# A graph attention and the routing behind it in one stage, with masks made on VectorE and each routed row written with both gates

## The reference

```python
x = x + _L2_gnn_ref(_layernorm(x), adj, W, a)      # graph attention
    h = x @ W;  e = s_src[:, :, None] + s_dst[:, None, :]   # h @ a[:d], h @ a[d:]
    e = where(e >= 0, e, 0.2 * e);  e = where(A <= 0, -inf, e)
    y = softmax(e) @ h
x = x + _L2_ffn_ref(_layernorm(x), ...)            # 8 experts, top 2
    probs = softmax(xt @ Wr + br);  top_p, top_idx = top_k(probs, 2)
    weights = top_p / top_p.sum(-1)
    xn = layernorm(xt)                             # a second norm
    out = sum of weights * (gelu(xn * g + b @ W1 + b1) @ W2 + b2) of the two experts
x = x + _L3_gnn_ref(_layernorm(x), adj, W, a)      # graph attention again
x = x + _L3_ffn_ref(...)                           # heads over 192 tokens, then 8 gated experts, top 2
```

## Time and profile before

| | us |
|---|---|
| median of 3 runs | 5281.62 |
| lowest, highest | 5274.88, 5283.15 |
| profiled execution | 5278.31 |
| its span | 5276.6 |

### The profile page before, as it was taken

The page is one execution under the profiler, slowest core; times in us unless marked ns, Lnnn a source line. Parts: engine busy times, 40 slices in busy tenths (PEclk is TensorE's granted clock), DMA queues, the critical chain, the costliest instruction groups (busy, mean ns, idle before and its releaser), DMA issues. The chain is left out here.

```text
span 5276.6 us, 85946 instructions
## 1 busy us (share of the span) xinstructions
PE 3931.5 (75%) x25676; PEld 2536.8 (48%) x25676; DVE 2964.8 (56%) x10714; ACT 2064.0 (39%) x5230; POOL 1883.7 (36%) x1833
## 2 busy tenths in 40 slices
PE   3999978888888539999886776279565677751995
PEld 1333337777777313333364565157454344431563
DVE  5666644444444766666487887412388555552344
ACT  1666643333333006566532265234255344431331
POOL 3445410000000024554362174745575311236344
PEclk9999975555555659999998888589888899965997
DMA  4333348000000023333100021144431000001445
GB/s 130 107 103 115 97 170 374 0 0 0 0 0 0 0 76 100 112 107 101 32 0 1 5 100 33 47 123 148 144 103 33 1 0 0 0 21 49 130 128 160
DMA packets 237303, 376.21 MB, mean 71 GB/s; under 512 B 24832, under 2 KB 157056, under 8 KB 228672
## 3 DMA queue, kind: packets, MB, share of 16 engines
q1 hardware_dynamic: 218688, 336.03, 20.3%
q0 software_dynamic: 18432, 38.05, 2.1%
HBM read 210.37 MB, written 163.61 MB: 71 GB/s over the span
## 5 line engine op out<-in xcount | busy, mean ns | idle before, releaser
L1343 DVE CUSTOM_DVE_ANT_0 mha_seen<-mha_score,mha_mask 128x512 f32<-128x512 f32 x1024 | 686.4, 688 | 456.5 <-PE mha_score L1114 453.4
L1246 ACT ACTIVATE mha_prob<-mha_turned 128x512 f32<-128x512 f32 x1024 | 608.8, 601 | 489.5 <-PE mha_turned L1125 459.1
L1114 PE MATMUL mha_score<-mha_k_rows,mha_q_rows 96*128 96x512 bf16 x1024 | 397.0, 390 | 58.3 <-DMA mha_k_rows<-split_rows 29.8
L3025 POOL DMA_INDIRECT expert_rows<-expert_y,expert_target x320 | 306.3, 957 | 368.4 <-DVE expert_y L3160 150.6
L1124 PE MATMUL mha_turned<-mha_maskT,core_ident_bf 128*128 128x512 bf16 x1024 | 392.4, 383 | 4.0 <-ACT mha_prob L1246 3.5
L1125 PE MATMUL mha_turned<-mha_q_rows,mha_k_rows 99*128 99x512 bf16 x1024 | 390.3, 381 | 0.0
L1498 PE MATMUL lstm_gates<-lstm_h_part,lstm_w_part 128*128 128x16 f16 x4608 | 271.4, 179 | 123.6 <-DVE lstm_h_part L1660 123.5
L1448 POOL TENSOR_TENSOR core_mid<-lstm_hist,lstm_per_unit 128x256 f32 x32 | 23.5, 733 | 942.8 <-DVE lstm_hist L1661 942.8
L1498 PEld LDWEIGHTS lstm_gates<-lstm_h_part,lstm_w_part 128*128 128x128 f16 x4608 | 231.2, 109 | 211.4 <-DVE lstm_h_part L1660 164.2
L1491 PE MATMUL lstm_gates<-lstm_xg,core_ident 128*128 128x48 f32 x1024 | 327.9, 420 | 0.7 <-ACT lstm_xg L1566 0.7
L2698 POOL DMA_INDIRECT routed_rows<-route_rows,core_slot x256 | 254.1, 993 | 149.8 <-issue 82.6
(11 more groups left out here) (477 smaller groups left out, 9282.3 us busy)
## 6 DMA issues: line engine op xcount, KB each, us to landing
routed_rows<-lstm_blank SPq DMA_DIRECT2D x66, 1040.0 KB, 25.0
core_params<-adj SPq DMA_DIRECT2D x32, 1024.0 KB, 5.9
gat_adj_raw<-adj SPq DMA_DIRECT2D x32, 1024.0 KB, 5.4
mha_q_rows<-split_rows SPq DMA_DIRECT2D x64, 384.0 KB, 4.5
mha_k_rows<-split_rows SPq DMA_DIRECT2D x64, 384.0 KB, 5.5
expert_x<-routed_rows SPq DMA_DIRECT2D x80, 260.0 KB
expert_w<-weights SPq DMA_DIRECT2D x80, 256.0 KB
combine_pair<-expert_rows SPq DMA_DIRECT2D x32, 512.0 KB, 4.9
```

The source lines that it names most:

```text
L1114: pe.matmul(score[n % 2][:, :], rows[0][s][0:ROWS, h, t * P:(t + 1) * P], rows[1][s][0:ROWS, h, :], start=True, stop=True).then_inc(S["sco ...
L1246: act.activation(prob[:, n % RING, :], turned[n % 2][:, :], ACT.Exp, scale=-1.0).then_inc(S["prob_ready"], 1)
L1343: dve.tensor_tensor_reduce(seen[n % 2][:, :], score[n % 2][:, :], mask[1 - s][:, t, :], 1.0, 3e38, ALU.add, ALU.min, low[g][:, t, j:j + 1] ...
L3025: pool.indirect_dma_start(out=core.y_rows[NUMBER][:, :], out_offset=bass.IndirectOffsetOnAxis(ap=target[q][:, t:t + 1], axis=0), in_=y_buf ...
```

## The change

- The first routing becomes part of the first graph attention: `gat_stage(core, 5, 2, route=6)`, with a class Router that holds the routing's steps. The loop over graphs runs 22 iterations instead of 16. In iteration b (where the index exists) POOL normalises graph b + 2, makes the scales of graph b - 1 (11 operations of 128x4, two of them powers, in place of DVE's bit trick over all graphs), and from iteration 6 on writes half a group, 8 DMAs, of group b // 2 - 3. PE turns and rates graph b - 2 between its attention matmuls; ACT scales the rows of graph b - 1 straight into the rows to be written. DVE makes the mask of b + 2, then the mark step of a group in odd iterations from 5, the pick step in even ones from 4, takes the logits of b - 2, then does out(b).
- Masks are made on DVE in both graph attentions, ahead by two graphs (L2671 of the changed kernel).
- zlow has one PSUM bank instead of two, in both graph attentions: ACT's lower of tile t waits for DVE's leak of tile t - 1. The other bank holds the counts.
- Each token has one row in SBUF, and both writes take it. ROW is 132: 128 features, the mark, the second slot's line, the lower gate, and the difference of the gates. The expert stages find out by comparing the line with their own index which of the two gates is meant (four more operations of 128x4 a tile on DVE, one iota and one addition at the start).
- The second routing loses copy_rows on ACT and the copy L2841 on DVE; ACT normalises into a ring of three groups.
- SP waits for four semaphores of written rows instead of two. The blanked buffer is larger by 132/130.

(In the diff: first the sizes and two of the Router's methods, then the buffers, the programs of POOL, PE, ACT and DVE in gat_stage in that order, then POOL in route_stage, DVE in expert_stage and the program.)

```diff
-ROW = D + 2
+ROW = D + 4
...
+    def scales(self, pool, b):
+        chain.step(pool.tensor_scalar(arg, var, LN_EPS, None, ALU.add))
+        chain.step(pool.tensor_scalar(shift, mean, -1.0, None, ALU.mult))
+        chain.settle()
+        chain.step(pool.tensor_tensor(scale, arg, half, ALU.pow))
+        chain.settle()
...
+    def normal(self, act, b):
+        act.wait_ge(S["r_scaled"], b + 1)
+        if g >= self.RING:
+            act.wait_ge(self.sent[s], 16 * 2 * self.R * (g // self.RING))
+        for t in range(T):
+            ins = act.activation(self.rows[s][:, i * T + t, 0:D], self.core.x_res[:, b, t, :], ACT.Identity, ...)
...
-        zlow = [m.ps(f"zlow{n}") for n in range(2)]
+        zlow, count_ps = m.ps("zlow"), m.ps("count_ps")
+        rate_ps = [s_ps[:, (2 + n) * T * E_:(3 + n) * T * E_] for n in range(2)]
+        router = Router(m, core, route, S) if route else None
+        LAST = B + 5 if route else B - 1
...
             need(pool, "stat_done", STATS[False])
             normalise(0)
-            forbid(0)
             normalise(1)
-            for b in range(B):
-                if b + 1 < B:
-                    forbid(b + 1)
+            if route:
+                router.constants(pool)
+            for b in range(LAST + 1):
                 if b + 2 < B:
                     normalise(b + 2)
+                if route and 0 <= b - 1 < B:
+                    need(pool, "stat_out", b)
+                    router.scales(pool, b - 1)
+                if route and b >= 6:
+                    half = b % 2 * T
+                    router.scatter(pool, b // 2 - 3, range(half, half + T))
...
+            for b in range(LAST + 1):
+                if route and 5 <= b < B + 5 and b % 2:
+                    router.count_picked(pe, (b - 5) // 2, count_ps)
+                if b < B:
+                    back(b, 0)
+                    back(b, 1)
+                    values(b, 0)
+                if routed:
+                    route_turn(b - 2)
+                if b < B:
+                    back(b, 2)
+                    values(b, 1)
+                if routed:
+                    route_rate(b - 2)
...
-                need(act, "leaky", T * b + t - 1)
+                need(act, "leaky", T * b + t)
...
+                if route and 0 <= b - 2 < B:
+                    router.take_turned(act, b - 2, row_ps)
...
+                if route and 0 <= b - 1 < B:
+                    router.normal(act, b - 1)
...
+            forbid(0)
+            forbid(1)
             masked(0)
...
                         leak(b + 1, t)
-                out(b)
+                if b + 2 < B:
+                    forbid(b + 2)
+                if route and 5 <= b < B + 5 and b % 2:
+                    router.mark_rows(dve, (b - 5) // 2, count_ps)
+                if route and 4 <= b < B + 4 and b % 2 == 0:
+                    router.pick(dve, b // 2 - 2)
+                if route and 0 <= b - 2 < B:
+                    router.take(dve, b - 2, rate_ps[b % 2])
+                    if b % 2:
+                        router.lower_logits(dve, (b - 3) // 2)
+                if b < B:
+                    out(b)
...
-                                                in_=out_rows[s][i][:, r, :], in_offset=None).then_inc(sent[s], 16)
+                                                in_=out_rows[g % 3][:, r, :], in_offset=None).then_inc(sent[g % 4], 16)
...
+                dve.tensor_tensor(upper[q][:, :], line, index[:, bass.ds(n, 1), :]..., ALU.is_equal)
+                dve.tensor_tensor(idle[q][:, :], idle[q][:, :], upper[q][:, :], ALU.add)
+                dve.tensor_tensor(gate[q][:, :], upper[q][:, :], more, ALU.mult)
+                dve.tensor_tensor(gate[q][:, :], gate[q][:, :], low_gate, ALU.add)
...
-    gat_stage(core, 5, 2)
-    route_stage(core, 6, True)
+    gat_stage(core, 5, 2, route=6)
```

More of the change, by code:

```diff
@@ L2117, in gat_stage @@
+def gat_stage(core, k, i, route=None):
     nc = core.nc
@@ L2229, in _ @@
                 project(b)
-            for b in range(B):
-                back(b, 0)
-                for t in range(1, T):
-                    back(b, t)
-                    values(b, t - 1)
+            for b in range(LAST + 1):
+                routed = route and 0 <= b - 2 < B
+                if route and 5 <= b < B + 5 and b % 2:
[12 more added lines that the diff above has]
+                if b < B:
+                    back(b, 3)
+                    values(b, 2)
                 if b + 2 < B:
                     rows_in(b + 2)
-                values(b, T - 1)
+                if b < B:
+                    values(b, T - 1)
                 if b + 2 < B:
@@ L2289, in _ @@
             project(1)
-            for b in range(B):
-                ahead = b + 1 < B
-                exponent(b, 1)
-                take(b, 0)
-                exponent(b, 2)
-                take(b, 1)
+            for b in range(LAST + 1):
+                inside, ahead = b < B, b + 1 < B
+                if route and 4 <= b < B + 4 and b % 2 == 0:
+                    router.exponents(act, b // 2 - 2)
+                if inside:
+                    exponent(b, 1)
+                    take(b, 0)
+                    exponent(b, 2)
+                    take(b, 1)
+                if route and 0 <= b - 2 < B:
+                    router.take_turned(act, b - 2, row_ps)
                 if ahead:
                     lower(b + 1, 0)
-                exponent(b, 3)
+                if inside:
+                    exponent(b, 3)
                 if ahead:
                     lower(b + 1, 1)
-                take(b, 2)
+                if inside:
+                    take(b, 2)
                 if ahead:
@@ L2305, in _ @@
                     rows_in(b + 2)
-                take(b, 3)
+                if inside:
+                    take(b, 3)
                 if ahead:
@@ L2320, in _, with forbid @@
             need(dve, "const_set", 2)
+            if route:
+                router.begin(dve)
+            def forbid(b):
+                s = b % 2
+                need(dve, f"adj_in{s}", 16 * (b // 2 + 1))
+                need(dve, "masked", T * (b - 1))
+                dve.tensor_scalar(mask[s][:, :, :], adj_raw[s][:, :, :], 0.0, -BIG, ALU.is_le if i == 2 else ALU.is_equal,
+                                  ALU.mult).then_inc(S["mask_ready"], 1)
             def masked(b):
@@ L2632, in route_stage @@
     R = GRAPHS * T
-    NUMBER = int(not renorm)
+    NUMBER = 1
     with ExitStack() as ctx:
@@ L2640, in route_stage @@
         stat = core.x_stat
-        source = core.x_res if renorm else core.mid
-        rstd, shift, inner = m.sb("rstd", [P, B, T]), m.sb("shift", [P, B, T]), m.sb("inner", [P, B, T])
+        source = core.mid
+        rstd, shift = m.sb("rstd", [P, B, T]), m.sb("shift", [P, B, T])
         scratch, term = m.sb("scratch", [P, B, T]), m.sb("term", [P, B, T])
-        xn = [m.sb(f"xn{s}", [P, R, D]) for s in range(2)]
-        out_rows = [[m.sb(f"rows{s}{i}", [P, R, ROW]) for i in range(2)] for s in range(2)]
+        out_rows = [m.sb(f"rows{s}", [P, R, ROW]) for s in range(3)]
         xT = [m.sb(f"xT{s}", [P, N]) for s in range(2)]
@@ L2823, in _ @@
                     got = lg[i][:, 0:T * E_].rearrange("p (t e) -> p t e", t=T)
[L2824 to L2828 removed]
+                    g_.step(dve.tensor_copy(out, got))
                 dve.sem_inc(S["xn_taken"], 1)
@@ L2973, in expert_stage @@
         idle = [m.sb(f"idle{q}", [P, G]) for q in range(QUEUE)]
+        index = m.sb("index", [P, TILES, G])
+        upper = [m.sb(f"upper{q}", [P, G]) for q in range(QUEUE)]
+        gate = [m.sb(f"gate{q}", [P, G]) for q in range(QUEUE)]
         xT = [m.sb(f"xT{s}", [P, WIDE]) for s in range(2)]
```

441 lines of the change are left out of this document (332 added, 109 removed).

## The result

The changed kernel took 5299.46 us in the median of 7 runs, the kernel before 5283.15 beside it: a ratio of 1.0029, 95% interval 1.0018 to 1.0040. It is slower by a little more than what can be told, where 5212 had been forecast. The profiled execution has a span of 5297.7 us, 21.1 more than before.

| stretch | before | after | difference | forecast |
|---|---|---|---|---|
| first attention's first mask addition of graph 1 | 3056.89 | 3055.38 | -1.5 | -3 |
| from there to the first load of routed rows | 402.5 | 427.7 | +25.2 | -44 |
| from there to the last attention's first adjacency load | 373.0 | 373.5 | +0.4 | 0 |
| last graph attention, from there to its last reciprocal | 215.8 | 212.2 | -3.6 | -14 |
| from there to the second load of routed rows | 829.0 | 828.7 | -0.3 | -5 |

What follows compares the result with a forecast made beforehand. DVE was taken to bound attention, POOL's writes with TensorE's pauses routing. From 5278.3 us, first attention with fused routing -47, last attention -14 and second routing -5 gave 5212; range 5165 to 5260, faster at 0.87.

Steps and rivals of the forecast that it cites:

- The 3.93 us hold of DVE by POOL's mask: Graph attention: POOL's mask holds up DVE's 128x4 addition 3.93 us in each graph; the change removes this.
- DVE's routing steps at 4.8 us a graph: Fused stage: routing's small steps plus taking and lowering of logits cost DVE about 4.8 us a graph.
- the late signals: Fused stage: pauses of TensorE beside POOL's writes add 3.0 us a graph, ending with a block of 8 writes.
- DVE needs 11.8 + 4.8 + 1.0 = 17.6: Steady fused graph: attention 11.8, routing steps 4.8, held up by POOL 1.0; 20.6 us with TensorE's pauses.
- In comes the mask on DVE ... 0.7 less a graph: Attention alone: 12.47 less 3.93, plus mask 1.22 and single zlow buffer 2.0, gives 11.8 us a graph.
- The single zlow bank, +2.0: Both graph attentions: the handshake of ScalarE and DVE on one buffer adds 2.0 us a graph (ends 0 and 2.6).
- Pauses at full length: Slower rival: each fused graph meets a 14.3 us TensorE pause and takes 31.9; +113 us, 5325; chance 0.09.
- TensorE at its lower level: Rival: TensorE at 1.2 GHz in the fused stage, 23.9 us a graph; +33 us, 5245; chance 0.13.
- The mask at 2.3: Rival: DVE's mask takes 2.3 us instead of 1.22, 1.08 more for 32 graphs; 5246; chance 0.10.
- no pauses: Rival: TensorE isn't held in the fused stage, POOL paces graphs at 18.1; 25 us less, 5187; chance 0.22.
- The second routing: Second routing: copies on DVE and ScalarE leave the chain; about -5 us (ends 0 and -20).
- The mask beside the writes: Fused stage: DVE's mask delaying POOL's writes costed at nothing, POOL having 2.5 us a graph to spare.

Runs made afterwards that it cites:

- rate_bank: Changed kernel with the router's logits in the counts' PSUM bank instead of the bank of s_ps; 5197.92 us, ratio 0.9905 to the kernel before.
- last_two_zlow: Changed kernel with two zlow banks in the last graph attention only; 5247.21 us, ratio 0.9999.
- take_first: Changed kernel with DVE taking the logits ahead of mask, pick and mark steps, bank still shared; 5244.27 us, ratio 0.9897.
- after_again: The changed kernel itself, unaltered, run again in a later series; ratio 1.0021 to the kernel before.
- best_a: Changed kernel with logits in the counts' bank, two zlow banks in the last attention, and ACT taking the turned rows later; 5173.99 us, ratio 0.9859.
- bank_both: Changed kernel with logits in the counts' bank, rows scaled on DVE instead of ACT, and turned rows taken later; 5241.57 us, ratio 0.9901.
- dve_mask_only: Kernel before with only the masks moved to DVE in both graph attentions, two graphs ahead; 5224.77 us, ratio 0.9958.
- bank_two_zlow: Changed kernel with logits in the counts' bank and two zlow banks in the last graph attention; 5192.75 us, ratio 0.9895.

## Why the prediction was wrong

**What held.** The 3.93 us hold of DVE by POOL's mask (gone), the mask at 1.22 (1.220 measured), a write at 1.27 to 1.32, DVE's routing steps at 4.8 us a graph (4.3 and 5.2 by turns, from the end of the mask to the reciprocal), the first experts' and gated experts' stages unchanged (+0.9 at most), the late signals: 3.0 a graph forecast, about 2.5 seen where there are any. That the late signals are let go when POOL stops writing was called a reading; the last section has the rows, and they agree.

**The step that failed: "DVE needs 11.8 + 4.8 + 1.0 = 17.6", taken as the length of a graph.** The sum counted DVE's instructions and POOL's and took the larger. It never asked what DVE's new steps stand in front of. The change adds a wait of TensorE's projection for the taking of the logits, and the taking stands behind mask and pick or mark steps. Behind that wait stand the projection, ACT's s_low and h, its scaling of rows, two exponents and copies, then zlow, for which DVE waits. The front part even names the order of these steps on DVE, but the prediction costed them at their own time. Undoing this one wait is worth 5.6 us a graph (rate_bank against last_two_zlow), up to 1.8 of it by TensorE's clock; putting the taking first is worth 6.4 (take_first against after_again), late signals included. Steady graphs were 5.8 over the forecast (26.4 against 20.6). Without ring and late signals rate_bank has 18.5 where the forecast had 17.6; the ring adds 5.6 where it had 0, and late signals about 2.5 where it had 3.0. That 17.6 comes so near 18.5 is partly luck, since the errors of the next two points stand in it with both signs.

**Second: "In comes the mask on DVE ... 0.7 less a graph", from DVE never resting.** It was true that DVE never rested, and the hold was real. But ACT and TensorE had a ring of 12.0 us just below DVE's 12.47, seen as ACT 8.6 busy and 3.4 of waits for TensorE once DVE is out of the way. Of 2.7 us (3.93 - 1.22) taken off DVE, 0.4 came out. The last attention gained 3.6 us, 2.9 of them at its start (3.5 forecast), where 14 had been forecast. The single zlow bank, +2.0, cost 0.3: an error of the other sign out of the same oversight.

**Third: ACT was not costed in the fused stage at all.** Scaling (1.65) and the turned rows (0.59 and a wait of 1.9) stand in that ring: iterations 2 and 3 took 16.4 and 17.4 where 12.3 and 12.8 had been forecast, without any write or pick. This makes +8.7 in these two; best_a and bank_both, which relieve ACT, have 14.6 and 15.0, 13.6 and 14.1.

The rest of the 69 us: graph 0 +2.4, iterations 4 and 5 +10.6 of the same causes, and the end: POOL had 56 writes left where 48 were forecast (+10.1), the first load of rows came 2.6 us later behind the last write than before, where the forecast said that this stays so, and the last two graphs were shorter (-11.5).

**The rivals.** Pauses at full length, the slower case, would have shown waits over 10 us; the longest is 4.5 there. The result lies near the turning point that this rival was given, a steady graph of 27.2: it was 26.4, with earlier iterations longer. That is a coincidence of numbers, since the graph got there by another mechanism. TensorE at its lower level came true in part: the granted clock was 0.70 in the fused stage, 0.86 in best_a, where the same work lies closer together. TensorE is busy for 126.0 us in the eight steady graphs of the changed kernel and for 97.7 in best_a, 3.5 a graph; how much of that lay on the path wasn't measured apart. The mask at 2.3 and "no pauses" are out, the second for this chip; in the first series it was so.

**The second routing** gained nothing, and not 5 us. From its first instruction to the first load of rows it took 208.3 us before and 210.5 after; the -0.3 of the table comes from the stages ahead of it, 2.5 shorter with no change in them. Its writes take 182.7 us from first to last before and 183.3 after, and DVE's waits for TensorE's counts are as long (44.7 us before, 43.9 after, three each). Where no signal is late, some of the gain shows: in dve_mask_only, which has the old routing, the stage takes 191.0 us and the writes 165.3, in last_two_zlow, which has the new one, 188.7 and 161.5. So 3.8 us come off the writes there, and the late signals cover them in the first pair. But 2.0 are lost behind them: from the last write to the load it is 7.0 us and not 5.0. SP waits for four semaphores there instead of two; whether that is the cause was not tested.

**The mask beside the writes.** The forecast costed it at nothing. In the changed kernel no mask falls into a block of writes, in the kernels with shorter graphs nearly each does. This is one in bank_both:

```profile
3233.65 0.96 POOL L2213 DMA_INDIRECT routed_rows<-gat_r_rows,core_slot  x1 [0.30 <-issue]
3234.92 1.60 POOL L2213 DMA_INDIRECT routed_rows<-gat_r_rows,core_slot  x1 [0.30 <-issue]
3235.18 1.22 DVE L2669 TENSOR_SCALAR gat_mask<-gat_adj_raw 128x2048 bf16<-128x2048 int32 x1
```

The write beside the mask takes 1.60 instead of 0.96 and ends 0.12 us after it (3236.52 against 3236.40). In rate_bank, bank_two_zlow and best_a it is the same 0.12 wherever a mask starts within the first 0.5 us of a write. If it starts later, from 0.53 us on, that write takes its 0.96, and the next one, issued beside the mask, ends 0.81 to 0.84 after it. The Trainium skill has this rule (SBUF — State Buffer, "SBUF: two separate sides"): the descriptors wait until DVE's end and about 115 ns, and the trace agrees for a write that had begun before the mask. The copy of the earlier trace rows is of the other kind:

```profile
4759.75 0.70 DVE L2841 COPY route_rows<-route_xn 128x1024 f32<-128x1024 f32 x1 [10.91 <-DMA routed_rows<-route_rows,core_slot]
```

The write at 4759.86 ends 0.82 after it, and so does the one beside the two-input operation of the earlier trace rows. The cost here is 0.4 to 1.1 us a graph on POOL, under the 1.3 that was estimated from the page.

## What to carry to other kernels

When two stages are laid side by side, add up each engine's work, but then walk round each new wait: what stands behind the instruction that waits, and who waits for that. Two engines at half load that hand work to each other in turn are a bound that no busy column shows. Before an engine that never rests is relieved, read how the others' waits would close up behind it: here another ring stood 0.4 us below. And where PSUM banks are shared, take the reader's step first, ahead of work that nobody waits for; one moved call was worth 64 us (5244.27 against 5308.45), a share of late signals in it.

## What the runs showed of the hardware

**Late signals.** While POOL issued indirect DMAs, ACT waited up to 4.5 us for TensorE's work that was recorded as done (5.6 in after_again), and DVE up to 16.4 in the routing of the kernel before. These waits end with POOL's writes. Of the eight of ACT in the fused stage, five ended 1.4 to 1.6 us after the last write of a block of 8 and three within 0.12 us of the end of a write; the seven at the same place in after_again ended 1.5 to 1.7 after the block's last write. DVE's five in the kernel before ended 0.0 to 4.6 us after the last write of a block of 16. What holds the signals stays open.

They seem to go by chip. Where the kernel before took 5283 and 5298 us, the second routing's writes took 183 and 186 us in the changed kernel; where it took 5247 and 5246, they took 161 and no wait is marked "remote". These last two series ran on one chip, half an hour apart, with the one at 5298 on another chip between them. The 22 us are more than half of the 36 between 5283 and 5247. Another 9 lie between the first load of routed rows and the last attention's first load: 373 us in the first runs, 363 to 365 on the quiet chip (383 where the kernel before took 5298). Steady fused graphs differ by 2.5 us.

**DVE and POOL.** On DVE the mask of 128x2048, int32 to bf16, takes 1.22 us alone; the first two of the fused stage took 3.94 together, beside POOL's norm of the first graphs, and the first of the last attention 1.62. POOL's addition of 128x512 beside it took 1.90 instead of 1.04. So each holds the other. How long the hold of the kernel before lasted is regular, too: in all 28 masks that POOL made with DVE's 128x4 addition behind it, the addition ended 4.5 us after the mask's start, whether it had begun 0.15, 0.4 or 1.0 us into it (4.35, 4.09 and 3.53 us), with 2.6 us of the mask left.
